# Key units evicted two ahead into four buffers, and a query unit's four rotations shared by DVE and POOL

## The reference

```python
q = _causal_conv1d(_causal_conv1d(q, qc1_w, qc1_b, N_HEADS), qc2_w, qc2_b, 1)
k = _causal_conv1d(_causal_conv1d(k, kc1_w, kc1_b, N_KV), kc2_w, kc2_b, 1)
q = q.reshape(B, S, N_HEADS, HEAD_DIM) + 0.5 * k_mean[:, :, None, :]
k = k.reshape(B, S, N_KV, HEAD_DIM) + 0.5 * q_mean[:, :, None, :]
...
q = _l2norm(q)                  # 16 heads of 64
k = _l2norm(k) * key_temp       # 4 heads of 64
q = _rope(q, cos, sin)          # x1*cos - x2*sin, x1*sin + x2*cos
k = _rope(k, cos, sin)
...                             # scores, softmax, values, w_o
```

## Time and profile before

| | |
|---|---|
| median of 3 runs | 2742.55 us (2742.53 to 2745.01) |
| the profiled execution: its time | 2741.31 us |
| its span | 2739.5 us |
| PE busy in the span | 2503.8 us, 91% |
| DVE busy | 1751.1 us, 64% |
| POOL busy | 1509.2 us, 55% |
| mean granted clock of TensorE | 0.963 |

### The profile page before, as it was taken

One profiled execution on the slowest core, in us unless ns is written; L12 is line 12 of the kernel. 1 busy time (PEld: TensorE's weight loads), 2 busy tenths in 40 slices (PEclk: granted clock), 3 DMA queues, 4 the chain that ended last, 5 costly groups with the idle time before them and its releaser, 6 DMA issues. The chain is left out here.

```text
span 2739.5 us, 37352 instructions
## 1 busy us (share of the span) xinstructions
PE 2503.8 (91%) x12664; PEld 1824.7 (67%) x12664; DVE 1751.1 (64%) x3146; ACT 1414.4 (52%) x2794; POOL 1509.2 (55%) x1299
## 2 busy tenths in 40 slices
PE   7989995899699779999999999999999999999948
PEld 3464443444487568878878877877877877877734
DVE  2053454576433767777777777777777777777764
ACT  2200003555221376676676676686676776776603
POOL 0053465454001238668668667677667777767641
PEclk9999998899799989999999999999999999999978
DMA  4012320000210253343342342342342352342210
GB/s 159 0 49 69 107 62 31 1 1 1 85 61 13 84 160 104 93 148 96 101 148 95 102 148 89 104 151 89 103 153 89 94 161 88 95 157 90 71 46 31
DMA packets 143483, 241.86 MB, mean 88 GB/s; under 512 B 28352, under 2 KB 48576, under 8 KB 143168
## 3 DMA queue, kind: packets, MB, share of 16 engines
q1 hardware_dynamic: 143296, 239.48, 27.7%
HBM read 232.08 MB, written 7.34 MB: 87 GB/s over the span
## 5 line engine op out<-in xcount | busy, mean ns | idle before, releaser
L1670 ACT ACTIVATE mix<-mix,sc 128x128 f32<-128x128 f32 x1024 | 310.9, 389 | 6.1 <-DMA sc<-head_scal 3.1
L98 PE MATMUL ps<-xt_hi,w_in_hi 128*128 128x512 f32 x640 | 269.6, 421 | 34.0 <-ACT sg L1660 29.6
L1840 DVE SCALAR_TENSOR_TENSOR feat<-ps,chan,feat 128x511 f32<-128x511 f32 (+2 forms) x384 | 284.1, 740 | 7.0 <-ACT feat L1650 5.3
L1988 POOL TENSOR_TENSOR w_in_lo<-w_in_raw,w_in_hi 128x512 fp32r<-128x512 f32 x158 | 213.3, 1350 | 135.1 <-ACT w_in_hi L1625 135.1
L1874 DVE TENSOR_TENSOR y_lo<-y,y_hi 128x512 fp32r<-128x512 f32 x128 | 174.9, 1366 | 159.7 <-ACT y_hi L1686 157.6
L1829 DVE TENSOR_TENSOR mix<-mix,cb 128x512 f32<-128x512 f32 x256 | 273.8, 1074 | 0.0
L1972 POOL TENSOR_TENSOR xend<-xdt,sc 128x384 f32<-128x384 f32 x128 | 107.3, 838 | 290.9 <-DVE xdt L1803 289.1
L99 PE MATMUL ps<-xt_lo,w_in_hi 128*128 128x512 f32 x640 | 256.0, 400 | 0.0
L100 PE MATMUL ps<-xt_hi,w_in_lo 128*128 128x512 f32 x640 | 255.7, 400 | 0.0
L98 PE MATMUL ps<-xt_hi,w_g_hi 128*128 128x512 f32 x512 | 214.9, 420 | 22.9 <-DVE feat L1840 22.9
L1517 PE MATMUL ps<-w_o_hi,y_hi 128*128 128x512 f32 x512 | 207.4, 405 | 5.1 <-DVE y_lo L1874 3.4
(11 more groups left out here) (270 smaller groups left out, 5975.9 us busy)
## 6 DMA issues: line engine op xcount, KB each, us to landing
mix<-row_cum SPq DMA_DIRECT2D x128, 512.0 KB, 5.7
w_in_raw<-in_w_conv_in SPq DMA_DIRECT2D x160, 256.0 KB, 3.2
w_g_raw<-in_w_gate_in SPq DMA_DIRECT2D x128, 256.0 KB, 3.3
ecb<-row_ecum SPq DMA_DIRECT2D x256, 96.0 KB, 3.3
w_o_raw<-in_w_out SPq DMA_DIRECT2D x64, 256.0 KB, 3.0
w<-in_w_c2q SPq DMA_DIRECT2D x16, 768.0 KB, 4.6
w<-in_w_c2q SPq DMA_DIRECT2D x16, 512.0 KB, 3.7
wqkv<-in_w_qkv SPq DMA_DIRECT2D x1, 3072.0 KB, 13.6
```

The source lines that it names most:

```text
L98: pe.matmul(out, a_hi, b_hi, start=(n == 0), stop=False)
L1670: last = act.activation(m, m, ACT.Relu, bias=sc[:, b, CUM, z, 2 * i + e:2 * i + e + 1], scale=-1.0)
L1840: dve.scalar_tensor_tensor(out=to, in0=ps[:, j % 2, 0:S - back], scalar=chan[:, bb % B, j, K1 - 1 - back:K1 - back], in1=to, op0=ALU.mult, ...
L1988: pool.tensor_tensor(w_in_lo[:, n % RING, :, :], w_in_raw[:, n % RING, :, :], w_in_hi[:, n % RING, :, :].bitcast(F32), ALU.subtract).then_ ...
```

## The change

Two edits in the middle block. In the first, `raw` gets four buffers (RAWK) and the eviction of key unit u + 2 stands ahead of `measure(u)` on DVE; units 0 and 1 are evicted ahead of the loop. In the second, POOL makes only the first two of the four products of a query unit (key units keep all four on POOL), and DVE makes the other two in `turn`, ahead of the subtraction and the addition. A new semaphore `late_rot` counts DVE's two, and `rot_done` counts POOL's, now two for a query unit.

```diff
-    NI = 4 * QT
+    NI, RAWK = 4 * QT, 4
...
-            raw = sb("raw", [P, 2, KV0, HD])
+            raw = sb("raw", [P, RAWK, KV0, HD])
...
+            def rots_before(u):
+                return 4 * min(u, NK) + 2 * max(u - NK, 0)
+
+            def rotate(eng, u, i, side, table):
+                kind, n, t, e = units[u]
+                heads = KV0 if kind == "k" else HF
+                pair = unit[:, u % 2, 0:heads, :].rearrange("p h (j e) -> p h j e", e=2)
+                which, z = (0, t % ZB) if kind == "k" else (1, t % 2 * 2 + e)
+                return eng.tensor_tensor(rot[:, i, 0:heads, :], pair[:, :, :, side],
+                                         table[:, which, z:z + 1, :].to_broadcast([P, heads, HD // 2]), ALU.mult)
...
                     def first(u):
                         dve.wait_ge(c2_ready, u + 1)
-                        if u >= 2:
-                            dve.wait_ge(sq_done, u - 1)
+                        if u >= RAWK:
+                            dve.wait_ge(sq_done, u - RAWK + 1)
...
                         if u >= 2:
-                            dve.wait_ge(rot_done, 4 * (u - 1))
+                            dve.wait_ge(rot_done, rots_before(u - 1))
+                            if u - 1 > NK:
+                                dve.wait_ge(late_rot, 2 * (u - 1 - NK))
...
-                        dve.wait_ge(rot_done, 4 * (u + 1))
                         dve.wait_ge(unit_done, u + 1)
+                        if kind == "q":
+                            for i, side, table in ((2, 0, sin), (3, 1, cos)):
+                                rotate(dve, u, i, side, table).then_inc(late_rot, 1)
+                            dve.wait_ge(late_rot, 2 * (u + 1 - NK))
+                        dve.wait_ge(rot_done, rots_before(u + 1))
                         for half, op in ((0, ALU.subtract), (1, ALU.add)):
...
                         dve.wait_ge(rope_loaded, 16 * 7)
+                        first(0)
+                        first(1)
                         for u in range(NK + 1):
+                            if u + 2 < NK:
+                                first(u + 2)
                             if u < NK:
-                                first(u)
                                 measure(u)
...
-                        for i, (side, table) in enumerate(((0, cos), (1, sin), (0, sin), (1, cos))):
-                            pool.tensor_tensor(rot[:, i, 0:heads, :], pair[:, :, :, side],
-                                               table[:, which, z:z + 1, :].to_broadcast([P, heads, HD // 2]),
-                                               ALU.mult).then_inc(rot_done, 1)
+                        turns = ((0, 0, cos), (1, 1, sin), (2, 0, sin), (3, 1, cos))
+                        for i, side, table in turns if kind == "k" else turns[0:2]:
+                            rotate(pool, u, i, side, table).then_inc(rot_done, 1)
```

More of the change, by code:

```diff
@@ L407, in attention @@
             rot_done = core.sem("a_rot_done")
+            late_rot = core.sem("a_late_rot")
             rope_done = core.sem("a_rope_done")
@@ L562, in first @@
                         dve.wait_ge(c2_ready, u + 1)
-                        if u >= 2:
-                            dve.wait_ge(sq_done, u - 1)
-                        dve.tensor_tensor(raw[:, u % 2, :, :].rearrange("p h d -> p (h d)"), ps[:, u % 4, 0:KVD], bk[:, :],
+                        if u >= RAWK:
+                            dve.wait_ge(sq_done, u - RAWK + 1)
+                        dve.tensor_tensor(raw[:, u % RAWK, :, :].rearrange("p h d -> p (h d)"), ps[:, u % 4, 0:KVD], bk[:, :],
                                           ALU.add).then_inc(raw_done, 1)
@@ L587, in scale @@
                             dve.wait_ge(rnt_done, u + 1)
-                            src, by = raw[:, u % 2, :, :], rnt
+                            src, by = raw[:, u % RAWK, :, :], rnt
                         else:
@@ L633, in square @@
                         if kind == "k":
-                            heads, src = KV0, raw[:, u % 2, :, :]
+                            heads, src = KV0, raw[:, u % RAWK, :, :]
                             act.wait_ge(raw_done, u + 1)
@@ L681, in rope @@
                             pool.wait_ge(rope_done, 2 * u)
-                        pair = unit[:, u % 2, 0:heads, :].rearrange("p h (j e) -> p h j e", e=2)
-                        which, z = (0, t % ZB) if kind == "k" else (1, t % 2 * 2 + e)
-                        for i, (side, table) in enumerate(((0, cos), (1, sin), (0, sin), (1, cos))):
-                            pool.tensor_tensor(rot[:, i, 0:heads, :], pair[:, :, :, side],
-                                               table[:, which, z:z + 1, :].to_broadcast([P, heads, HD // 2]),
-                                               ALU.mult).then_inc(rot_done, 1)
+                        turns = ((0, 0, cos), (1, 1, sin), (2, 0, sin), (3, 1, cos))
+                        for i, side, table in turns if kind == "k" else turns[0:2]:
+                            rotate(pool, u, i, side, table).then_inc(rot_done, 1)
                     def rope_k():
```

## The result

The changed kernel takes 2731.23 us (median of 5 runs, 2730.38 to 2734.56), the kernel before 2742.55 (5 runs, 2742.03 to 2745.01): 0.9958 of the time, 95% interval 0.9945 to 0.9972, so 11.3 us or 0.4% less. 2732.1 was forecast. The two profiled executions have spans of 2739.5 and 2729.4 us, 10.1 apart.

What follows compares the result with a forecast made beforehand. Time could come only from PE's gap before the first query item and the tail behind its last matmul. Gains of 2.6 and 7.8 us, 10.4 in all, took 2742.55 to 2732.1 us; range 2727.5 to 2736.0.

Steps and rivals of the forecast that it cites:

- The sum: Whole kernel: 2.6 us from the earlier key evictions plus 7.8 from the shorter tail, 10.4 us gained.
- the round of `rope_k`: Key part: a round stays at 3.48 us, made by POOL; evicting earlier only changes which round evicts unit 7.
- the block's start to item 2: Front: item 2 on PE, bound by DVE's `mixed`, begins 5.0 us earlier, bounds 5.0 and 6.0.
- the delay of 0.4 us by the three evictions: Key part: `measure(0)` stands behind three evictions, the third needing the third unit, so later rounds come 0.4 us later.
- The middle: Middle of the query part: DVE's two products, up to 0.85 us, hide in its wait for `rn`; nothing gained.
- the tail: Chain of DVE and POOL behind the first output tile's eviction: 7.8 us shorter, bounds 6.0 and 8.6.
- signs of being wrong: Wrong if DVE's products exceed 0.9 us, `rope_k` rounds exceed 3.5, or PE shows gaps between 310 and 420.
- The clock: PE's gap before item 2: TensorE falls to 1.2 GHz, costing 2.4 us, the middle of 1.5 and 3.3.
- rival A: PE's two front gaps: clock falls in neither or only the first; gain 12.8, time 2729.7 us; chance 0.25.
- count of gaps: PE's trace before: 14 gaps of 1.9 to 3.8 us beginning at 2.4 GHz, clock falling behind 10, staying behind 4.
- Rival C: Tail: DVE's products wait for POOL's, about 1.1 us each, a pair about unchanged; 2738.9 us; chance 0.08.
- D: Tail: each DVE product costs 1.7 us beside POOL, slower from 1.3 on; about 2750 us; chance 0.04.

Runs made afterwards that it cites:

- bias first: Changed kernel with DMAs of key bias and temperature issued ahead of the cos and sin tables, first evictions waiting only for those two: 2730.97 us.

## Why the prediction was right, and where not

The sum was 10.4 us, the median moved by 11.3 and the trace by 10.1 (and by 9.4 in the second session of the same two kernels). That the sum came so near is in part luck, as the terms below show. Right as steps: the round of `rope_k` stayed at 3.47 us (evictions at 181.37 and 184.84), unit 7 was evicted two rounds earlier, PE then stood before item 2 waiting for `mixed`, and `mixed` took 2.35 and not 1.28, since POOL went on to the next `tx` at once. From the block's start to item 2 the gain is 4.1 us, with the first eviction 1.0 us later than it should be by the block's start: 5.1 against 5.0 in the sum. Of the delay of 0.4 us by the three evictions only 0.1 came (the last key unit's `unit` stands 27.49 us behind the first eviction, 27.40 before): with the tables late, the third key unit was long out of PE. The middle hid DVE's products, and PE had no gap there but the wait for weights, 0.3 us longer than before.

**Mis-sized: the tail**, 7.8 in the sum, 6.2 measured, with 6.0 as the lower bound. I went nearer the upper end "since only the last unit starts both at the same moment". They need not start together: in each second unit DVE's first product met POOL's second, which took 0.99 for 0.74, and this met DVE's second, which took 0.95 for 0.42; `rn` behind them took 1.81 for 1.63, and the unit 4.27 and not 3.84. One of the forecast's own signs of being wrong, products over 0.9 us each, thus came for 5 of the tail's 18 products on DVE; the others took 0.41 to 0.43. PE's last gap is 18.66 and not 17. Against the upper bound of 8.6 the seven steps from unit to unit lost 4 x 0.43 + 3 x 0.06 = 1.9 us, and the last unit gained 0.9 (447.69 to 452.07 before, 439.73 to 443.22 after) and not 1.4. The first units, at 4.73, were right to 0.06. The kernel with three products on DVE, in which none meet, has 3.40.

**The clock** was forecast to fall at the second gap for 2.4 us. In both traces of the changed kernel it fell at the first, where it cost nothing: rival A's case. The forecast had the second gap at 4.6 us, and this goes with a clock that stays up at the first. In the three traces of that kind (three products, one product, bias first) items 0 and 1 took 13.97 us, the second gap was 4.53 to 4.55, and the clock fell at it in all three. In the three others with the same front (the two of the changed kernel, the first edit alone) the clock fell at the first gap, items 0 and 1 took 15.55 to 15.67, the second gap shrank to 2.85 to 2.96, and the clock fell at it in one, that of the first edit alone. Six traces are few, and nothing here decides which of the two an execution will be. Where it fell at the second gap, item 2 took 1.6 to 2.3 us longer: so the term is real, comes in some executions, and was taken 0.1 to 0.8 too high. That the sum still came out is luck: this term was paid in 0 us, while the tail gave 1.6 less and the tables came 1.0 late.

The forecast's count of gaps was off as well. The trace of before has 20 gaps of 1.9 to 3.8 us that begin at 2.4 GHz, not 14, and the clock goes down behind 16 of them, not 10. And the gap before 2723.16, its example of a clock that stays, begins at 1.2 GHz, at 2721.25:

```profile
2721.00:2721.50 0.50, 0.24 (x1) 0.50 0.00 0
```

The clock rose in it. With 16 of 20 the forecast's choice of a fall was better founded than it knew.

**Not seen: the late tables.** From the first issue of the seven small DMAs to the first eviction it is 8.50 and 8.54 us in the two traces of before, and 9.1 to 10.5 in the eight traces of changed kernels that keep the order of these DMAs. One of the issues, mostly the first for `sin`, takes 1.1 to 2.2 us where most take 0.4 to 0.5, in before as well. That is only part of it: the seven issues take 4.3 us in all in both traces of before and 4.5 to 5.2 in the eight, and from the end of the last one to the first eviction it is 4.2 us in before and 4.4 to 5.3 in the eight. Eight to two is hardly chance, but no run here separates which part of the program does it, and the cause stays open. That it was on the path is shown by the kernel with the bias first, whose item 2 came 0.8 and 1.7 us earlier behind the first issue.

Rival C (about 1.1 us a product) would have left a last gap of about 24; D needed 1.3 us: no product took more than 0.96. Between products of both engines the one that began first kept its time and the other ended later: DVE's at 418.91 took 0.41 and POOL's from 418.93 took 0.99; DVE's next, from 419.25, took 0.96. Both came only some 0.13 us sooner than if they had waited for the whole of the other and then taken their usual 0.74 and 0.42. Under `rn` there was no such wait: with three products on DVE, those from 419.54 to 420.63 took 0.41 to 0.42 each, nearly all of it beside the `rn` of 419.70 to 421.44. The Trainium skill describes a lock on a shared pair of ports in "SBUF — State Buffer" ("SBUF: two separate sides"): who starts first gets it for the whole instruction, and the other blocks. The trace agrees, but for those 0.13 us, between the products, and does not for `rn`.

## What to carry to other kernels

When a wait is taken away, look at once for the next thing that the engine needs: here it was the preparation of the third item, one round later, and evicting two ahead gained no more than one ahead. In a chain that passes through two engines, to shift work pays by what it takes off the slower leg, and where the pieces fall in time counts too: two plus two products met each other, one plus three did not (no run here changed the placing and kept the amount). Two short gaps in place of a long one can bring TensorE's clock down twice, and what a fall costs depends on what PE next waits for: ahead of items 0 and 1 it cost nothing, at item 2 up to 2.3 us. So compare several traces before a gain of 2 us in such a place is believed.

## What the hardware showed that was not expected

An elementwise product of DVE (128x256, 0.42 us) and one of POOL (0.74) that overlap don't share the loss: the first to begin keeps its time, and the other ends later, with 0.95 for DVE's or 0.99 for POOL's. In the last unit, where they start together, POOL's took 0.97 and 0.91 and DVE's 0.42 and 0.96. POOL's power (`rn`, 1.74 us) doesn't hold DVE's products up at all. And seven small DMAs issued in a row by SyncE do not take an even time: one of the issues, in one kernel two, takes 1.1 to 2.2 us where the others take 0.3 to 0.7, and not the same one in every kernel.
